# The square root of a variance, spread over channels by GpSimd through HBM instead of by TensorE

## The reference

```python
x = layernorm2d(x0, ln_w, ln_b)            # over the 96 channels of each pixel
qk = conv1x1(x, qk_w, qk_b)                # 48 channels of q, 48 of k
vs = conv1x1(x, vs_w, vs_b)
local = depthwise_3x3(vs) + depth_b
# q, k, v1 shifted by 4, windows of 8x8, 4 heads of 12 channels
y = concat([softmax(q k^T * SCALE) v1, v2])
s = (y + local).mean(over the image)       # gate: needs a whole image
ca = sigmoid(fu2 @ leaky_relu(fu1 @ s, 0.2))
z = proj(y * ca + local * (1 - ca)) + proj_b + x0
# second layer: 3x3 filters (upper 4 taps) made from the image's pooled z
out = depthwise_masked_3x3(z, filters(mean(z))) + bias
```

## Time and profile before

| what | us |
|---|---|
| median of 3 runs | 1415.69 (1414.25 to 1417.43) |
| profiled execution, its own time | 1415.28 |
| profiled execution, span from first to last instruction | 1413.6 |
| mean granted TensorE clock | 0.989 of full |
| PE busy | 1303.9 (92%) |
| DVE busy | 1174.8 (83%) |
| ACT busy | 953.1 (67%) |
| POOL busy | 398.3 (28%) |

### The profile page before, as it was taken

The page is one execution under the profiler, slowest core; times in us unless marked ns, Lnnn a source line. Parts: engine busy times, 40 slices in busy tenths (PEclk is TensorE's granted clock), DMA queues, the critical chain, the costliest instruction groups (busy, mean ns, idle before and its releaser), DMA issues.

```text
span 1413.6 us, 38309 instructions
## 1 busy us (share of the span) xinstructions
PE 1303.9 (92%) x12403; PEld 773.8 (55%) x12403; DVE 1174.8 (83%) x2028; ACT 953.1 (67%) x2375; POOL 398.3 (28%) x870
## 2 busy tenths in 40 slices
PE   5999999899999999999999999989999999679995
PEld 3666667655555555555555555555555555323331
DVE  3566656579999999999999999999999999779996
ACT  2576766777777777787777777777777777533332
POOL 3121211123333333333333332333333332111111
PEclk9999999999999999999999999999999999899998
DMA  2122222455666766666666655665667665568995
GB/s 66 51 86 64 80 68 76 111 132 138 151 161 171 164 154 155 150 166 153 149 160 171 169 154 150 151 166 148 158 152 174 165 155 149 132 156 209 222 228 135
DMA packets 81364, 203.13 MB, mean 144 GB/s; under 512 B 15248, under 2 KB 19112, under 8 KB 81320
## 3 DMA queue, kind: packets, MB, share of 16 engines
q1 hardware_dynamic: 72424, 176.65, 47.8%
q0 software_dynamic: 7168, 25.17, 9.6%
q10 hardware_dynamic: 1728, 0.79, 0.2%
HBM read 136.57 MB, written 64.91 MB: 143 GB/s over the span
## 4 chain that ended last, share of the span: by engine, by line
PE 36%; DVE 22%; DMA 15%; ACT 13%; issue 9%; ACTq 2%; SPq 1%; POOLq 0%; DVEq 0%; POOL 0%
DMA zs<-in_x 12%; DVE mixed L1273 7%; PE banks_g L532 7%; PE banks_s L557 5%; PE banks_g L645 5%; DVE mx L1099 4%; ACT zs L904 4%; PE banks_t L591 3%; ACT vd L843 3%; DMA ycat<-y_img 3%; PE banks_g L540 3%; DVE oo L1285 3%; DVE xn L1092 3%; PE banks_t L565 2%; DVE bn L1071 2%
## 5 line engine op out<-in xcount | busy, mean ns | idle before, releaser
L1273 DVE SCALAR_TENSOR_TENSOR mixed<-vin,c_pack,mixed 96x1024 f32<-96x1024 f32 x352 | 451.1, 1282 | 8.6 <-ACT mixed L893 1.6
L1285 DVE SCALAR_TENSOR_TENSOR oo<-zs,l_w,oo 96x1016 f32<-96x1016 f32 x192 | 243.8, 1270 | 46.4 <-ACT oo L914 42.5
L447 POOL COPY vrow<-vw 96x16 f32<-96x16 f32 (+2 forms) x520 | 265.2, 565 | 0.0
L467 POOL TENSOR_TENSOR rest<-rest 96x1 f32<-96x1 f32 x64 | 38.5, 601 | 605.4 <-ACT zs L904 605.4
L1099 DVE TENSOR_REDUCE mx<-banks_s 128x16 f32<-128x1024 f32 x130 | 158.4, 1218 | 23.1 <-PE banks_s L557 22.0
L1071 DVE BATCH_NORM_STATS2 bn<-banks_a 128x6 f32<-128x96 f32 x528 | 99.7, 251 | 85.1 <-PE banks_a L507 84.7
L557 PE MATMUL banks_s<-km,qd 64*128 64x128 f32 x2080 | 152.9, 287 | 14.5 <-DVE mx L1099 12.8
L557 PEld LDWEIGHTS banks_s<-km,qd 64*128 64x128 f32 x2080 | 128.4, 189 | 67.4 <-ACT qd L827 34.6
L645 PE MATMUL banks_g<-vin,proj_t 128*96 128x512 f32 (+1 forms) x288 | 149.0, 618 | 13.4 <-DMA ycat<-y_img 6.6
L867 ACT ACTIVATE pt<-banks_t 128x512 f32<-128x512 f32 x256 | 137.6, 589 | 34.8 <-PE banks_t L565 34.8
L565 PE MATMUL banks_t<-qd,km 64*128 64x128 f32 x2048 | 150.5, 287 | 3.3 <-DMA qd<-nmx 3.3
(11 more groups left out here) (151 smaller groups left out, 1817.4 us busy)
## 6 DMA issues: line engine op xcount, KB each, us to landing
vin<-v_img SPq DMA_DIRECT2D x64, 495.0 KB, 5.6
v_img<-vrow SPq DMA_DIRECT2D x130, 198.0 KB, 2.7
xc<-in_x SPq DMA_DIRECT2D x134, 192.0 KB, 7.0
zs<-in_x POOLq DMA_DIRECT2D x64, 384.0 KB, 8.7
out<-oo SPq DMA_DIRECT2D x64, 384.0 KB, 3.5
y_img<-ybuf SPq DMA_DIRECT2D x128, 99.0 KB, 2.0
ycat<-v_img SPq DMA_DIRECT2D x64, 198.0 KB, 4.9
ycat<-y_img SPq DMA_DIRECT2D x64, 198.0 KB, 7.9
```

Source lines behind the costliest of these rows:

```text
L447: nc.gpsimd.tensor_copy(dst.rearrange("c r (p x) -> c p r x", x=min(WS, src.shape[-1])), src).then_inc(vrow_done, 1)
L1273: v.scalar_tensor_tensor(out=mb[:C, par, :, 0:W], in0=vin[:C, par, 1 + dh:1 + dh + WS, 1 + dw:1 + dw + W], scalar=depth_w[:, DVE_TAPS[m]:D ...
L1285: v.scalar_tensor_tensor(out=oo[:, par, :, to], in0=zs[:, par, 1 + dh:1 + dh + WS, of], scalar=l1_w[:, tap:tap + 1], in1=oo[:, par, :, to] ...
```

## The change

In all joined strips (16 to 63) the eight transposes of `rstd` and their read from PSUM are replaced. PE transposes `var` once to [8, 128] (`var_row`, behind keys and queries, in front of values half 0). ACT takes Ln and Exp of that (`rsqrt_row`, now behind keys and in front of queries). GpSimd, behind `to_image`, makes a mark (an addition on the new tile `mark`) and begins a DMA of the 4 KB to HBM (`store_row`); it waits for it, makes a second mark and begins a DMA that reads the 4 KB back into each of 96 partitions (`spread_row`), 384 KB; `wrap` comes behind. DVE multiplies both chunks from SBUF in `normalise_all`, which now stands behind divide 1, in front of l1 steps 2 and 3. Strips 0 to 15 keep the old way.

Steps are moved as well. On DVE, mix 5 goes in front of maxima 0, the gate steps `gates` and `projections` behind mix 3. On PE, rows (`project_rows` of chunk 0) join the taps in front of scores 0, and values half 1 goes in front of scores 1; the gate's second column goes behind `var_row`. On ACT the gate's exponential goes behind the root.

```diff
+            def store_row(s, par):
+                pool.wait_ge(row_turn, FREE + 2 * (s - LAG - 1))
+                pool.wait_ge(rstd_done, s + 1)
+                nc.gpsimd.tensor_tensor(mark[:], mark[:], mark[:], ALU.add).then_inc(row_turn, 1)
+                pool.dma_start(r_img[par, :, :], rstd_row[:]).then_inc(row_stored, 16)
+
+            def spread_row(s, par):
+                pool.wait_ge(row_stored, 16 * (s - LAG))
+                pool.wait_ge(row_turn, FREE + 2 * (s - LAG) - 1)
+                pool.wait_ge(xn_done, 2 * s)
+                nc.gpsimd.tensor_tensor(mark[:], mark[:], mark[:], ALU.add).then_inc(row_turn, 1)
+                pool.dma_start(rstd_all[:].rearrange("c a n -> c (a n)"),
+                               r_img[par, :, :].rearrange("j p -> (j p)").unsqueeze(0).to_broadcast([C, WS * 128])
+                               ).then_inc(row_spread, 16)
@@ GpSimd, strip
                     to_image(t + 1, 1 - k, h + k)
+                    if joined:
+                        store_row(t + 2, k)
+                        spread_row(t + 2, k)
                     wrap(t + 2)
@@ TensorE
+            def var_row(s):
+                pe.wait_ge(var_done, s + 1)
+                nc.tensor.transpose(ps_ln[:WS, 0:128], var[:], ident[:]).then_inc(var_turned, 1)
...
+                if attend:
+                    keys_queries(t + 1)
+                    var_row(t + 2)
                 if gated is not None and attend:
                     one_column(gated, fu2T[:], tr[:, 1:2], 2, C, 2)
                 if attend:
-                    keys_queries(t + 1)
                     values(t, k, 0)
-                    rstd_rows(t + 2, 0)
-                    rstd_rows(t + 2, 1)
                     pe.wait_ge(km_done, 2 * (t + 2))
...
-                    project_taps(u, um, par, 0, tail)
+                    project(u, um, par, 0, tail)
...
-                if cur:
-                    project_rows(par, 0, tail)
...
-                    pe.wait_ge(xn_done, 2 * (t + 2) + 1)
+                    pe.wait_ge(pt_done, 4 * (t + 1))
                     y_transposed(t - 1, 1 - k)
+                    values(t, k, 1, spread=True)
                     pe.wait_ge(mx_done, 2 * (t + 1) + 1)
                     scores(1 - k, 1)
-                    values(t, k, 1)
@@ ScalarE
+            def rsqrt_row(s):
+                act.wait_ge(var_turned, s - LAG)
+                fn(ln_rows[:], ps_ln[:WS, 0:128], ACT.Ln, bias=eps[:WS, 0:1]).then_inc(ln_done, 1)
+                act.wait_ge(ln_done, s + 1)
+                act.wait_ge(row_turn, FREE + 2 * (s - LAG - 1))
+                fn(rstd_row[:], ln_rows[:], ACT.Exp, scale=-0.5).then_inc(rstd_done, 1)
...
                     exps(t, 1)
+                    keys(t + 1, 1 - k)
+                    rsqrt_row(t + 2)
                     if gated is not None:
                         sigmoid_exp(gated)
-                    rsqrt(t + 2)
-                    keys(t + 1, 1 - k)
                     queries(t + 1, 1 - k)
@@ VectorE
+            def normalise_all(s, par):
+                dve.wait_ge(row_spread, 16 * (s - LAG))
+                dve.wait_ge(kq_done, 2 * s)
+                for c in range(2):
+                    v.tensor_tensor(xn[:, 4 * c:4 * c + 4, 0:W], chunk(rstd_all[:, c, :]), chunk(xc[:, par, c, :]),
+                                    ALU.mult).then_inc(xn_done, 1)
...
+                if cur:
+                    mix(u, par, 3, tail)
                 if gated is not None and attend:
                     gates(gated)
                     projections(gated)
-                if cur:
-                    mix(u, par, 3, tail)
                 if cur and not tail:
                     mix(u, par, 4, tail)
                 if attend:
                     divide(t, k, 0)
-                    normalise(t + 2, k, 0)
-                    normalise(t + 2, k, 1)
+                if cur and not tail:
+                    mix(u, par, 5, tail)
+                if attend:
                     maxima(t + 1, 0)
...
-                if cur and not tail:
-                    mix(u, par, 5, tail)
...
                     divide(t, k, 1)
+                    normalise_all(t + 2, k)
```

## The result

The changed kernel takes **1504.9 us** (median of 4 runs, 1502.6 to 1519.6) against 1416.6 us for the kernel before in the same comparison: a ratio of 1.065, 95% interval 1.060 to 1.070. That is 88 us more where 53 were forecast, inside the range and on the forecast's side. The profiled execution spans 1499.8 us against 1413.6.

The account below looks back on a forecast made before the run. PE and DVE nearly fill the joined strips; the root's path through GpSimd and HBM makes DVE wait, so strips go from 19.6 to 20.8 us: 44 x 1.2 = 52.8 us on 1415.3 gives 1468 us, range 1393 to 1517.

Parts of the forecast that it names:

- V: The moment in a strip when var is done and DVE's mix 2 begins; the forecast's times count from it.
- step 6: DVE's normalise_all, 1.2 us plus 0.05 wake-up, ending at V + 13.3; without the wait it would begin at V + 9.8.
- steps 6 and 7: From the read back's landing to the next V: normalise_all and wake-up, then 7.56 us of l1, statistics and mixes.
- Step 5: The read back of 384 KB into 96 partitions: 3.6 us, landing at V + 12.0.
- Steps 1 and 2: GpSimd ends to_image's copies at V + 4.3, then makes store_row's mark and issues the store at V + 4.6.
- This end is tied to V: Step 1's claim that GpSimd's last copy, or the mark behind it, always stands behind mix 4, ending at V + 3.9.
- Step 3: The root's 4 KB store to HBM: 2.5 us, landing at V + 7.1.
- P: The moment in a strip when PE starts the vs matmuls.
- Step 4: spread_row's mark on GpSimd, held behind l1 step 1 until V + 8.0, with the read back issued at V + 8.4.
- I let these cancel: Strips beside gates: small DVE steps in the stall offset up to 1.3 us more for ACT's projections, three times.
- both transfers quick: Rival, chance 0.21: store lands by V + 6.6, read back 3.5 us, strip 19.1 us, kernel 1393 us.
- PE's floor of 18.9: The shortest strip PE's work allows after the change, 0.7 us less than before.

Follow-up runs that it names:

- l1 first: The changed kernel with DVE issuing l1 steps 2 and 3 ahead of normalise_all in strips without a gate; 1422.0 us, ratio 1.003.
- marks that only write: The changed kernel with both GpSimd marks a memset behind a semaphore increment instead of an addition; 1504.4 us, ratio 1.060.
- old root, moves kept: The changed kernel with the root by eight transposes and multiplications from PSUM again, all other moves of the change kept; 1447.5 us, ratio 1.019.
- filler: The kernel with l1 steps 2 and 3 ahead of normalise_all, plus 12 more variance transposes on PE in gate strips; 1421.4 us, ratio 1.002.

## Why the prediction was right, and where it was off

**The path was right.** DVE waits in normalise_all for the read back, nothing covers it, and l1, the statistics and the next mixes follow late. The wait begins at V + 9.85; step 6 had V + 9.8. From the end of the wait to the next V 8.72 us pass (762.45 to 771.17), in steps 6 and 7 1.25 + 7.56. The multiplications from SBUF take 684 ns against 677 from PSUM. To price the two multiplications from SBUF like those from PSUM was right.

**Step 5 was right:** 3.7 us, with 3.6 forecast. That 96 reads of one 4 KB row might be slow was named as the main risk; they aren't.

**Steps 1 and 2 were wrong for this kernel.** "This end is tied to V" failed as to where: the copies ended at V + 1.5 and the store was issued at V + 2.6, not V + 4.6. When DVE is late, GpSimd's copies run in the stretch of statistics and variance, where no mix holds them: 2.99 us instead of 5.05. Step 1 did say that more copies pass earlier if V falls later, and then kept the last one behind mix 4. With DVE not late the two steps are right within 0.2 us: in the run with l1 first the copies take 5.05 us, the mark 0.19, and the store is issued at V + 4.4.

**Step 3 is the term that was mis-sized.** Store 2.5 us; measured 6.0 in the joined stage, and 6.7 from its issue to the mark behind it in the strip shown. The prediction had the cause in hand ("its burst slides some 2 us against P, toward the store") and put it in the range instead of the term. It kept the burst's end at V + 7.2 and let a store issued at V + 4.6 land at V + 7.1, just as the burst ended. The store is issued earlier and lands later, at V + 9, because the burst now ends there; issued 0.7 us earlier still, it lands no sooner, as the marks that only write showed. Where the burst is mostly out of the way, 2.4 to 2.7 us are what the store takes. The Trainium skill (DMA: Bandwidth & Descriptors, the anatomy of a GpSimd DMA) gives about 2.0 us plus bytes over 436 GB/s, by this, an estimate, 2.0 us for the 4 KB. The 2.4 us of the run with l1 first are near it; the 6.0 us under the burst are not.

**Step 4** fell away: the mark took 0.19 us at the median, since the store landed after l1 step 1 had ended. From landing to the read back's issue 0.4 us pass instead of 1.3.

**The sum.** In the strip shown: issue -2.0, store and landing +4.2, mark -0.9, read back +0.1, later steps -0.1, that is 22.1 instead of 20.8 us. On average it is 21.36, so per plain strip the forecast's +1.2 was +1.7. The errors of steps 1, 3 and 4 hide each other in part, so the sum came out nearer than its terms: that much was luck.

**Strips beside gates: "I let these cancel" was wrong** by 14 us. There the small steps of DVE and ACT are on PE's path, PE waits for them up to 2.8 us where it waited 0.9, and its clock falls to half. The prediction also left the clock at 1.00. It had "PE's new slack of 2 us would cover a little of a loss"; it did not look at what more waiting does in a strip where the waits are already the longest. That the new root brings this on is shown (23.4 us with the old root, moves kept). It is not the wait for the store (28.4 us without it). Whether it is the lateness of DVE, or of ACT with its queries and proj_t, or PE's smaller work stays open.

**The rival "both transfers quick"** priced a strip at 19.1 us. With l1 first a case near to it is real (store 2.4, read 3.5, strip 19.29), if by another order on DVE. It gives no 1393 us: a plain strip gains 0.36 us and not 0.5, which is 15 us in all, and the two gate strips take 13 of them back. PE's floor of 18.9 was right, too: the shortest strips there are 18.8.

## What to carry to other kernels

In this kernel a small store cost what the DMA engines were busy with when it was issued: it landed about when the burst ended, whether it was issued early or late. So put both the issue and the burst of the kernel after on one axis, against the same event (V here), and take the landing from the burst's end there, not from where it ended before. Ask which queue's burst starts behind the very engine that will wait for the store. Where a wait on one engine can't be removed, move in front of it what other queues are waiting for: two instructions of l1 gave back 83 of 88 us. And strips with an irregular edge (gates, ends) need a price of their own: the longer waits there can bring the clock down, and then the matmuls behind them take up to twice as long.

## What the runs showed of the hardware

- A 4 KB store took 2.4 to 2.7 us at the end of SP's burst or behind it, and 6.0 when it was issued in the middle, with the DMA engines' share near 1.00. 384 KB read as 96 copies of one 4 KB row took 3.5 to 3.7 us, as much as out<-oo before, a plain store of the same size (3.5).
- GpSimd's one-column addition took 0.19 us alone and up to 1.20 beside DVE's mixes; a memset of the same column 0.09 to 0.10 us in all 89 cases from 330 to 1300 us.
- While TensorE stood for 2.59 us the granted clock went from 1.00 to 0.50, stayed there for 12 us more, and 16 matmuls took 3.64 instead of 1.92 us. The length of a single wait did not decide it: 1.08 us had half the clock behind it (l1 first), 1.68 us had the full one (old root, moves kept), and 1.44 and 1.43 us in one execution had the one and the other (filler).
- In the kernel before, waits of up to 0.94 us beside the gates of images 1 and 2 had no such fall behind them.
